# The first batch's selective scans in wide units of 1024 columns, their three elementwise steps all on VectorE

## The chip, the cores and the metric

One core of a Trainium2 chip runs the whole kernel in one launch. The metric is the device time of that launch in microseconds (us). The engines are TensorE (PE, matmul), VectorE (DVE), ScalarE (ACT), GpSimd (POOL) and SyncE (SP, which here only issues DMAs). Each engine takes its instructions in the order in which they were written for it, and they wait for one another by semaphores.

## The reference

The input is `x` (4 batches of 512 tokens, 256 wide) and a context (4 x 1601 x 256). One decoder layer is computed: a Mamba block, a cross-attention of 16 heads in which the context and the latents are keys and values, and a mixture of experts; after each a residual sum and a layernorm. The part that matters here is the Mamba scan:

```python
xs = silu(conv(xs) + conv_b);  dt = softplus(dt @ W_dt.T + b_dt)
dA  = exp(dt[..., None] * A)                      # 512 channels x 16 states x 512 tokens
dBx = dt[..., None] * Bm[:, :, None, :] * xs[..., None]
h_t = dA_t * h_(t-1) + dBx_t                      # recurrence over the 512 tokens
y_t = sum over the 16 states of h_t * C_t;   y = (y + xs * D) * silu(z) @ W_out.T
```

The attention needs `layer_norm(context) @ Wkv` and `layer_norm(x after Mamba) @ Wq`, in a precision near fp32: every weight is split into a high part and the rest (`raw - high`), and a product is the sum of three.

## The kernel before, in words

Three blocks follow each other: `mamba` (projections, convolution, dt; it leaves dt, dt*x, B, C and the gate in DRAM), `attention` and `experts`. The scans aren't done in `mamba`: each batch's scans run inside `attention`. Those of the next three batches run beside the attention of the batch before, on POOL and DVE, and nothing of them changes here. Those of the first batch (called batch 0 here) have no attention to run beside, and fill the opening of the `attention` block, from the first loads to the first scores. This opening is what the change touches.

A unit of a scan is one state n (of NS = 16) and one tile c of 128 channels (of CT = 4): 128 partitions x 512 tokens, so NU = 64 units a batch. A unit takes: `decays` on ACT (L833: exp of dt times a scale per partition), `times_b` on POOL (L731: dt*x times the row B_n), `scan` on DVE (L942: the recurrence, then from L953 the product with the row C_n, in place, unless `on_pool(u)`; for u = 24, 26, ... that product is `times_c` on POOL, L741), and `sum_state` on PE (L1208: one fp32 matmul with the identity, which adds the unit to the sum of its channel tile in PSUM). Rings of buffers: FR = 3 for decays and dbx each, FS = 4 for the states. The scan of unit u waits for the sum of unit u - FS. The rows B_n and C_n are one tile `bc` of 2 buffers, broadcast from DRAM by SP (`load_bc`).

The order of all that is one list written out by `first()` (L370), which every engine walks, each making its own part of an item: D (decays, times_b), H (scan), C (times_c, the sum), and between them the preparation of the context, in equal steps: S (row statistics, DVE), A (their sums, DVE, and a power on POOL), N (normalise two row tiles, DVE), T (turn them, PE, and high part, ACT), U (low part, DVE), W (split one weight, `split` at L761: both halves on POOL; 12 of them), then V and K (products of the context, PE, evicted by DVE, for K by ACT and DVE). There are 57 such items, the last nine V0 to V5 and K0 to K2. In the split, the first write of every third weight waits until SP has stored the tile of the split weights before it in DRAM (`w_stored`).

After the list's scans: `gate_first` (DVE, L958, it waits for the last sums and for the gate's DMA), the output projection, layernorms, Q and the remaining K, the first row maxima, and from there the attention of all heads.

Of the kernel before, what the change touches and what calls it, by code (L numbers as in the profile page):

```python
# [22 lines left out]
P = 128  # L23
# [9 lines left out]
KEPT = {}  # L33
# [268 lines left out]
FR = 3  # L302
FS = 4
# [4 lines left out]
NU = CT * NS  # L308
# [61 lines left out]
def first():  # L370


    early = [("S", 0, t) for t in range(CTX_T)] + [("A", 0, i) for i in range(2)]
    early += [("W", 0, i) for i in range(3 * NG)]
    n_ctx = CTX_T // 2 + 1
    for i in range(n_ctx + 1):
        early += ([("N", 0, i)] if i < n_ctx else []) + ([("T", 0, i - 1)] if i > 0 else [])
        early += [("U", 0, i - 2)] if i > 1 else []
    early += [("U", 0, n_ctx - 1)]
    early += [("V", 0, i) for i in range(V_EARLY)] + [("K", 0, i) for i in range(3)]  # L380

    splits, others = [x for x in early if x[0] == "W"], [x for x in early if x[0] in "SANTU"]
    head = []
    for i, x in enumerate(others):
        head += [x] + (splits[i // 2:i // 2 + 1] if i % 2 == 1 else [])
    head += splits[len(others) // 2:]
    early = head + [x for x in early if x[0] in "VK"]
    made, done = [], 0
    for u in range(NU + 3):
        for kind, later in (("H", 1), ("D", 0), ("C", 2)):  # L390
            if 0 <= u - later < NU:
                made.append((kind, 0, u - later))
        while done < len(early) and done * (NU - 4) < (u + 1) * len(early):
# [21 lines left out]
def attention(nc, ctx_rows, g1, b1, g2, b2, wq, wkv, wo, x1):  # L415
    w_dram = nc.dram_tensor("a_w_split", (NG, P, 6 * KD * GW), F32, kind="Internal").ap()

    with ExitStack() as ctx:
# [39 lines left out]
        decay_first, dbx_first, state_first = parts(early, 0, FR), parts(early, FR, FR), parts(early, 2 * FR, FS)  # L458
        w_out_first = early[:, (2 * FR + FS) * S:(2 * FR + FS + 2) * S].rearrange("p (c d) -> p c d", d=DM)
# [53 lines left out]
        seen_pool = sem("a_seen_pool")  # L513
        seen_dve = sem("a_seen_dve")
# [31 lines left out]
        def unit(b, u):  # L546
            return b * NU + u
# [4 lines left out]
        def on_pool(u):  # L552

            return u >= 24 and u % 2 == 0

        def by_pool(u):
            return sum(on_pool(i) for i in range(u + 1))

        def ring_of(b):
            return FR if b == 0 else 2  # L560

        def dtu_of(b, c, i):
            if c < 2:
                return dtu[:, c, i]
            return p[:, 2 * (c - 2) + i] if b == 0 else dtu_two[:, 2 * (c - 2) + i]

        def inputs(b, u):
            i = u % ring_of(b)
            return (decay_first[:, i], dbx_first[:, i]) if b == 0 else (decay[:, i], dbx[:, i])

        def state_of(b, u):
            return state_first[:, u % FS] if b == 0 else state[:, u % 2]

        def wait_inputs_free(engine, b, u):
            r = ring_of(b)
            if u >= r:
                engine.wait_ge(scanned, unit(b, u) - r + 1)
            elif b > 0:
                engine.wait_ge(turned_low, b * len(PREP))

        def wait_multiplied(engine, b, u):
            if b > 0:
                engine.wait_ge(seen_ready, late(b, u) + 1)
            else:
                if by_pool(u):
                    engine.wait_ge(seen_pool, by_pool(u))
                engine.wait_ge(seen_dve, u + 1 - by_pool(u))

        @block.sync
        def _(sp):  # L590
# [17 lines left out]

            def load_bc(b, n):
                i = b * NS + n  # L610
                if n >= 2:
                    wait_multiplied(sp, b, CT * (n - 1) - 1)
                elif b > 0:
                    sp.wait_ge(gated, b * CT)
                sp.dma_start(bc[:, i % 2].rearrange("p i s -> p (i s)"),
                             KEPT["bc"][BATCHES[b], n].partition_broadcast(P)).then_inc(bc_loaded[i % 2], 16)

            def load_gate(b):
                wait_multiplied(sp, b, NU - 1)
                sp.dma_start(gate.rearrange("p c s -> p (c s)"), KEPT["z"][BATCHES[b]]).then_inc(gate_loaded, 16)  # L620
                if b > 0:
                    sp.wait_ge(scanned, unit(b, NU))
                sp.dma_start(w_out_first if b == 0 else w_out,
                             KEPT["w_out_t"].rearrange("(c p) d -> p c d", p=P)).then_inc(w_out_loaded, 16)
# [23 lines left out]
            load_bc(0, 0)  # L648
            load_batch(0)
            load_rows(0)  # L650
            load_bc(0, 1)
# [4 lines left out]
            for what in BEFORE:  # L656
                if what[0] == "W" and what[2] >= 1 and what[2] + 1 < 3 * NG:
                    load_raw(what[2] + 1)
                elif what[0] == "W" and what[2] == 3 * NG - 1:
                    sp.wait_ge(raw_split, 3 * NG)  # L660
                    sp.dma_start(w_dram[0], wt[:].rearrange("p i k n -> p (i k n)").bitcast(F32)).then_inc(w_stored, 16)
                elif what[0] == "C" and what[2] % CT == CT - 1 and what[2] // CT + 2 < NS:
                    load_bc(0, what[2] // CT + 2)
# [46 lines left out]
        def _(pool):  # L710
# [20 lines left out]
            def times_b(b, u):  # L731
                n, c = divmod(u, CT)
                i = b * NS + n
# [5 lines left out]
                nc.gpsimd.tensor_tensor(inputs(b, u)[1], dtu_of(b, c, 1), bc[:, i % 2, 0], ALU.mult).then_inc(dbx_ready, 1)  # L739

            def times_c(b, u):  # L741
                n, c = divmod(u, CT)
                i = b * NS + n
                if b == 0:
                    if on_pool(u):
                        pool.wait_ge(scanned, u + 1)
                        nc.gpsimd.tensor_tensor(state_of(b, u), state_of(b, u), bc[:, i % 2, 1], ALU.mult).then_inc(seen_pool, 1)
                    return
# [23 lines left out]
            for what in BEFORE:  # L772
                if what[0] == "D":
                    times_b(*what[1:])
                elif what[0] == "C":
                    times_c(*what[1:])
                elif what[0] == "W":
                    split(what[2])
                elif what in POW:
                    make_rstd(what)  # L780
# [12 lines left out]
        def _(act):  # L793
# [39 lines left out]
            def decays(b, u):  # L833
                n, c = divmod(u, CT)
                wait_inputs_free(act, b, u)
                if u == 0:
                    act.wait_ge(dtu_loaded, 32 * (b + 1))
                nc.scalar.activation(inputs(b, u)[0], dtu_of(b, c, 0), ACT.Exp,
                                     scale=a_neg[:, c, n:n + 1]).then_inc(decay_ready, 1)

# [4 lines left out]
            def make(what):  # L845
# [6 lines left out]
                elif what[0] == "D":  # L852
                    decays(*what[1:])
# [30 lines left out]
        def _(dve):  # L884
            dve.wait_ge(a_set, 1)
            nc.vector.tensor_scalar(a_neg[:], a_neg[:], -1.0, None, ALU.mult).then_inc(a_set, 1)
            dve.wait_ge(consts_set, 1)
            nc.vector.memset(wo_sb[DH:DH + 1], 0.0)
# [53 lines left out]
            def scan(b, u):  # L942
                n, c = divmod(u, CT)
                i = b * NS + n
                dve.wait_ge(decay_ready, unit(b, u) + 1)
                dve.wait_ge(dbx_ready, unit(b, u) + 1)
                if b == 0 and u >= FS:
                    dve.wait_ge(summed, u - FS + 1)
                elif b > 0 and u >= 2:
                    dve.wait_ge(y_added, late(b, u) - 1)  # L950
                dA, dB = inputs(b, u)
                nc.vector.tensor_tensor_scan(state_of(b, u), dA, dB, 0.0, ALU.mult, ALU.add).then_inc(scanned, 1)  # L952
                if b == 0 and not on_pool(u):  # L953
                    dve.wait_ge(bc_loaded[i % 2], 16 * (i // 2 + 1))
                    dve.wait_ge(scanned, u + 1)
                    nc.vector.tensor_tensor(state_of(b, u), state_of(b, u), bc[:, i % 2, 1], ALU.mult).then_inc(seen_dve, 1)

            def gate_first():  # L958
                dve.wait_ge(y_loaded, 16)
                dve.wait_ge(gate_loaded, 16)  # L960
                for c in range(CT):
                    dve.wait_ge(summed, NU - CT + c + 1)
# [90 lines left out]
            def make(what):  # L1053
# [15 lines left out]
                elif kind == "H":  # L1069
                    scan(*what[1:])  # L1070
# [28 lines left out]
        def _(pe):  # L1099
# [108 lines left out]
            def sum_state(u):  # L1208
                wait_multiplied(pe, 0, u)
                n, c = divmod(u, CT)  # L1210
                nc.tensor.matmul(sums(c), ident[:], state_first[:, u % FS], start=(n == 0), stop=(n == NS - 1)).then_inc(summed, 1)

# [817 lines left out]
```

## Time and profile before

| | |
|---|---|
| median of 3 runs | 3302.6 us (3299.16 to 3303.39) |
| profiled execution, its own time | 3303.27 us |
| its span | 3301.5 us |
| busy over the span | PE 91%, DVE 62%, ACT 41%, POOL 33% |
| mean granted TensorE clock | 0.943 |

The span is the time from the first to the last instruction; the own time of the execution is 1.8 us more. Busy shares are means over stages with different limits: PE is nearly full from the first scores on, but not in the opening, which lies between about 199.8 us (first product of the scans) and 435 us (last product with C).

### The profile page before, as it was taken

To read this page: it belongs to the slowest core of one execution; us is meant where nothing else is said; L and a number is where in the kernel's file an instruction comes from. 1 tells how busy PE (TensorE), PEld (TensorE's weight loads), DVE (VectorE), ACT (ScalarE), POOL (GpSimd) and SP (SyncE) were. 2 spreads that over 40 slices of the span, in tenths; PEclk is the share of its full clock that TensorE was granted. 3 is DMA by queue.
4 is the path that set the end of the run, shared out by engine and by line. 5 is a ranking of instruction groups with operands and counts; after the bars stand their busy time and mean duration, and the time that the engine had idled before them with its cause. 6 is when DMAs were issued, how large, how long until landed. Compare 5 with 4: busy or idle time off the path is not lost. (4 is left out here: it accounts for less than half of the span.)

```text
span 3301.5 us, 33908 instructions
## 1 busy us (share of the span) xinstructions
PE 3000.6 (91%) x11590; PEld 1862.5 (56%) x11590; DVE 2040.4 (62%) x3415; ACT 1346.4 (41%) x2307; POOL 1084.0 (33%) x824
## 2 busy tenths in 40 slices
PE   6624659999999999999999999999999999899997
PEld 2201326656566665656565665666566665576666
DVE  4668867776756777775677777565555545352225
ACT  4521215454535445453645445344434344321121
POOL 0047726676500466660036666200000000102213
PEclk8856769999999999999999999999999999799998
DMA  2342122121212212121122112110101100321112
GB/s 100 122 157 89 57 88 77 33 61 33 61 34 58 80 37 68 33 61 41 36 71 68 54 34 62 53 36 14 36 14 43 36 18 16 129 81 48 52 41 69
DMA packets 73182, 189.83 MB, mean 57 GB/s; under 512 B 8388, under 2 KB 42312, under 8 KB 64440
## 3 DMA queue, kind: packets, MB, share of 16 engines
q1 hardware_dynamic: 69176, 178.37, 17.8%
q0 software_dynamic: 3408, 9.31, 1.0%
q8 instruction: 95, 1.56, 0.2%
q14 instruction: 71, 0.58, 0.1%
q10 hardware_dynamic: 432, 0.01, 0.0%
HBM read 120.39 MB, written 32.64 MB: 46 GB/s over the span
## 5 line engine op out<-in xcount | busy, mean ns | idle before, releaser
L1253 PE MATMUL a_o<-a_p,a_vals 128*65 128x512 f32 (+1 forms) x2176 | 1113.5, 593 | 0.0
L860 ACT ACTIVATE a_p<-a_st 128x512 f32<-128x512 f32 (+1 forms) x1088 | 649.2, 597 | 1127.1 <-PE a_st L1241 1119.0
L1018 DVE TENSOR_REDUCE a_maxes<-a_mx 128x1 f32<-128x512 f32 x1024 | 683.0, 686 | 219.6 <-PE a_mx L1171 213.1
L1241 PE MATMUL a_st<-a_q,a_kone 65*128 65x512 f32 (+1 forms) x1088 | 430.6, 396 | 0.0
L750 POOL TENSOR_TENSOR a_shared<-a_shared,a_bc 128x512 f32<-128x512 f32 x192 | 252.6, 1316 | 383.5 <-DVE a_shared L952 383.5
L1253 PEld LDWEIGHTS a_o<-a_p,a_vals 128*65 128x65 f32 (+1 forms) x2176 | 284.3, 137 | 103.4 <-issue 1.8
L1240 PE MATMUL a_st<-a_q,a_keven 128*128 128x512 f32 (+1 forms) x544 | 326.0, 599 | 0.7 <-issue 0.7
L1240 PE MATMUL a_st<-a_q,a_kodd 128*128 128x512 f32 (+1 forms) x544 | 314.7, 578 | 0.0
L729 POOL TENSOR_TENSOR a_erstd<-a_emv,a_half 128x4 f32<-128x4 f32 x8 | 8.1, 1014 | 916.1 <-DVE a_emv L1044 916.1
L1171 PE MATMUL a_mx<-a_kodd,a_q 128*128 128x512 f32 x512 | 298.3, 599 | 7.3 <-DVE a_maxes L1018 6.2
L952 DVE TENSOR_TENSOR_SCAN a_shared<-a_shared 128x512 f32<-128x512 f32 x192 | 287.7, 1500 | 13.1 <-POOL a_shared L739 12.0
L1171 PE MATMUL a_mx<-a_keven,a_q 128*128 128x512 f32 x512 | 277.0, 588 | 12.9 <-DVE a_maxes L1018 10.2
L1241 PEld LDWEIGHTS a_st<-a_q,a_kone 65*128 65x128 f32 (+1 forms) x1088 | 202.1, 186 | 152.8 <-issue 128.7
L754 POOL TENSOR_TENSOR a_y<-a_y,a_shared 128x512 f32<-128x512 f32 x192 | 255.6, 1331 | 15.3
L1124 PE MATMUL a_ring<-a_kvh,a_wt 128*128 128x512 f32 (+1 forms) x768 | 229.7, 381 | 5.1 <-DVE a_kvl L984 2.9
L1011 DVE COPY a_vals<-a_ring 128x512 f32<-128x512 f32 (+2 forms) x160 | 97.3, 608 | 186.4 <-PE a_ring L1124 184.3
L739 POOL TENSOR_TENSOR a_shared<-a_dtu,a_bc 128x512 f32<-128x512 f32 x96 | 146.6, 1528 | 169.2 <-DMA a_bc<-m_kept_bc 169.2
L1171 PEld LDWEIGHTS a_mx<-a_keven,a_q 128*128 128x128 f32 x512 | 97.9, 191 | 162.9 <-DVE a_maxes L1018 64.6
L1124 PE MATMUL a_ring<-a_wt,a_kvh 128*128 128x256 f32 (+1 forms) x1088 | 177.6, 286 | 0.0
L1240 PEld LDWEIGHTS a_st<-a_q,a_keven 128*128 128x128 f32 (+1 forms) x544 | 101.4, 186 | 132.5 <-issue 94.2
L1660 DVE TENSOR_TENSOR e_gate<-e_silu,e_h 128x512 f32<-128x512 f32 x71 | 48.7, 687 | 199.1 <-ACT e_silu L1522 180.0
L1124 PEld LDWEIGHTS a_ring<-a_wt,a_kvh 128*128 128x128 f32 (+1 forms) x1088 | 160.1, 189 | 18.4 <-issue 3.8
(243 smaller groups left out, 4539.7 us busy)
## 6 DMA issues: line engine op xcount, KB each, us to landing
a_bc<-m_kept_bc SPq DMA_DIRECT2D x64, 512.0 KB, 3.7
a_wt<-a_w_split SPq DMA_DIRECT2D x15, 1536.0 KB, 9.8
a_kone<-a_keven SPq DMA_DIRECT2D x32, 528.5 KB, 4.5
a_kone<-a_kodd SPq DMA_DIRECT2D x32, 528.5 KB, 4.2
e_wall<-in_w_t_dram SPq DMA_DIRECT2D x27, 512.0 KB, 5.5
a_shared<-in_ctx_dram SPq DMA_DIRECT2D x4, 1536.0 KB
a_w_split<-a_wt SPq DMA_DIRECT2D x4, 1536.0 KB, 8.5
e_y_dram<-e_y_row SPq DMA_DIRECT2D x39, 128.0 KB, 1.7
```

Source lines behind the costliest of these rows:

```text
L739: nc.gpsimd.tensor_tensor(inputs(b, u)[1], dtu_of(b, c, 1), bc[:, i % 2, 0], ALU.mult).then_inc(dbx_ready, 1)
L750: nc.gpsimd.tensor_tensor(state[:, u % 2], state[:, u % 2], bc[:, i % 2, 1], ALU.mult).then_inc(seen_ready, 1)
L754: nc.gpsimd.tensor_tensor(y[:, c], y[:, c], state[:, u % 2], ALU.add).then_inc(y_added, 1)
L860: nc.scalar.activation(p[0:r, s % 4], st[0:r, s % 2], ACT.Exp, scale=SCALE).then_inc(exp_done, 1)
L952: nc.vector.tensor_tensor_scan(state_of(b, u), dA, dB, 0.0, ALU.mult, ALU.add).then_inc(scanned, 1)
L1011: o = nc.vector.tensor_copy(vals[0:r, t * HG:(t + w) * HG, 0:DH], made)
L1018: nc.vector.reduce_max(maxes[:, c, t:t + 1], mx[:, i % 2], AX_X).then_inc(mx_max, 1)
L1124: mm = nc.tensor.matmul(out, x(k), y(k), start=(j == 0), stop=(j == len(terms) - 1))
L1171: mm = nc.tensor.matmul(mx[:, i % 2], qd[of(g)][:, t * P:(t + 1) * P], kk[:, c * 512:(c + 1) * 512], start=True, stop=True)
L1240: nc.tensor.matmul(st[0:r, s % 2], keys_of(g)[:, kt * P:kt * P + r], qd[of(g)], start=True, stop=False)
L1241: nc.tensor.matmul(st[0:r, s % 2], k_one[g % 2][0:DH + 1, kt * P:kt * P + r], qm[of(g)][0:DH + 1, :], start=False, stop=True).then_inc(st_ ...
L1253: nc.tensor.matmul(ps_o[0:DH + 1, g % 2], vals[0:r, kt * HG + j, :], p[0:r, s % 4], start=(kt == 0), stop=(kt == KT - 1)).then_inc(pv_done, 1)
```

## The change

The 64 units become NW = 32 wide units of CW = 2 channel tiles each: one state, 1024 columns, scanned as one (the decay of the first token of each half is a constant zero, so that the second half starts from zero). Both products are on DVE: that with B writes straight into the state's buffer, and the scan works there in place. The rings are FR = 2 wide decays, FS = 3 wide states and FB = 3 rows of B and C. The split's high half goes to ACT, POOL keeps the low half. On PE a wide unit has two matmuls and one semaphore step. The list has D, H, C and the same 57 items in the same order, spread over 32 rounds.

```diff
-FR = 3
-FS = 4
+NU = CT * NS
+CW = 2
+NW = NU // CW
+FR = 2
+FS = 3
+FB = 3
...
-    for u in range(NU + 3):
-        for kind, later in (("H", 1), ("D", 0), ("C", 2)):
-            if 0 <= u - later < NU:
-                made.append((kind, 0, u - later))
-        while done < len(early) and done * (NU - 4) < (u + 1) * len(early):
+    for w in range(-1, NW + 1):
+        made += [("D", 0, w + 1)] if w + 1 < NW else []
+        made += [("H", 0, w)] + ([("C", 0, w - 1)] if w > 0 else [])
+        while done < len(early) and done * (NW - 2) < (w + 2) * len(early):
...
+            def load_bc_first(n):
+                if n >= FB:
+                    sp.wait_ge(seen_first, CW * (n - FB + 1))
...
             def split(i):
                 which = i % 3
-                if which == 0 and i > 0:
-                    pool.wait_ge(w_stored, 16 * (i // 3))
-                pool.wait_ge(raw_loaded[i % 2], 16 * (i // 2 + 1))
+                pool.wait_ge(raw_high, i + 1)
                 raw = o_sb[:, i % 2].rearrange("p (k n) -> p k n", n=GW)
-                nc.gpsimd.tensor_copy(wt[:, 2 * which], raw).then_inc(raw_high, 1)
-                pool.wait_ge(raw_high, i + 1)
...
+            def decays_first(w):
+                n, k = divmod(w, CW)
+                if w >= FR:
+                    act.wait_ge(scanned, w - FR + 1)
...
+                for i in range(CW):
+                    c = k * CW + i
+                    e = nc.scalar.activation(decay_first[:, w % FR, i, 1:S], dtu_first(k, 0)[:, i, 1:S], ACT.Exp,
+                                             scale=a_neg[:, c, n:n + 1])
+                e.then_inc(decay_ready, 1)
+
+            def split_high(i):
+                which = i % 3
+                if which == 0 and i > 0:
+                    act.wait_ge(w_stored, 16 * (i // 3))
+                act.wait_ge(raw_loaded[i % 2], 16 * (i // 2 + 1))
+                nc.scalar.activation(wt[:, 2 * which], o_sb[:, i % 2].rearrange("p (k n) -> p k n", n=GW),
+                                     ACT.Copy).then_inc(raw_high, 1)
...
+            def scan_first(w):
+
+                if w + 1 < NW:
+                    n, k = divmod(w + 1, CW)
+                    if w == -1:
+                        dve.wait_ge(dtu_loaded, 32)
+                    if k == 0:
+                        dve.wait_ge(bc_first[n % FB], 16 * (n // FB + 1))
+                    if w + 1 >= FS:
+                        dve.wait_ge(summed, w + 1 - FS + 1)
+                    nc.vector.tensor_tensor(state_first[:, (w + 1) % FS], dtu_first(k, 1),
+                                            rows_first(n)[:, 0:1].to_broadcast([P, CW, S]), ALU.mult).then_inc(dbx_first, 1)
+                if 0 <= w < NW:
+                    dve.wait_ge(decay_ready, w + 1)
+                    dve.wait_ge(dbx_first, w + 1)
+                    h = state_first[:, w % FS].rearrange("p c s -> p (c s)")
+                    nc.vector.tensor_tensor_scan(h, decay_first[:, w % FR].rearrange("p c s -> p (c s)"), h, 0.0, ALU.mult,
+                                                 ALU.add).then_inc(scanned, 1)
+                if w >= 1:
+                    dve.wait_ge(scanned, w)
+                    h = state_first[:, (w - 1) % FS]
+                    nc.vector.tensor_tensor(h, h, rows_first((w - 1) // CW)[:, 1:2].to_broadcast([P, CW, S]),
+                                            ALU.mult).then_inc(seen_first, 1)
...
+            def sum_state(w):
+                wait_multiplied(pe, 0, w)
+                n, k = divmod(w, CW)
+                for i in range(CW):
+                    mm = nc.tensor.matmul(sums(k * CW + i), ident[:], state_first[:, w % FS, i], start=(n == 0), stop=(n == NS - 1))
+                mm.then_inc(summed, 1)
```

## Rows read from the trace of the kernel before

**Rows 1.** The page's busy times over the whole span.
```profile
PE 3000.6 (91%) x11590; PEld 1862.5 (56%) x11590; DVE 2040.4 (62%) x3415; ACT 1346.4 (41%) x2307; POOL 1084.0 (33%) x824
```

**Rows 2.** Windows view (PE, PEld, DVE, ACT, POOL busy, PE clock, DMA): the scans, then early attention.
```profile
204.00:435.00 231.00, 125.89 (x241) 48.40 (x242) 200.84 (x167) 56.22 (x88) 166.87 (x106) 0.65 0.23 74
...
520.00:540.00 20.00, 20.00 (x74) 11.95 (x73) 12.56 (x15) 14.35 (x25) 17.04 (x12) 1.00 0.07 27
```

**Rows 3.** Groups by line and shape, 195 to 440 us (busy, mean ns, idle before, releasers).
```profile
L952 DVE TENSOR_TENSOR_SCAN a_early<-a_early 128x512 f32<-128x512 f32 x64 | 109.7, 1724 | 18.8 <-POOL a_early L739 8.7 <-issue 6.9 <-ACT a_early L838 2.9
L956 DVE TENSOR_TENSOR a_early<-a_early,a_bc 128x512 f32<-128x512 f32 x44 | 58.3, 1326 | 4.6
L1211 PE MATMUL a_st<-a_early,a_ident 128*128 128x512 f32 x64 | 55.3, 970 | 89.3 <-DVE a_early L956 66.0 <-POOL a_early L747 23.1
```

**Rows 4.** Timeline, first units (start us, us, engine, line).
```profile
203.89 0.43 DVE L905 BATCH_NORM_STATS2 a_stats<-a_shared 128x6 f32<-128x256 f32 x1 [10.90 <-DMA a_shared<-in_ctx_dram]
204.23 1.21 DVE L952 TENSOR_TENSOR_SCAN a_early<-a_early 128x512 f32<-128x512 f32 x1
...
205.54 0.69 DVE L956 TENSOR_TENSOR a_early<-a_early,a_bc 128x512 f32<-128x512 f32 x1
...
206.38 4.24 PE L1211 MATMUL a_st<-a_early,a_ident 128*128 128x512 f32 x4 [43.31 <-DVE a_early L956]
```

**Rows 5.** Timeline near 251 us: DVE while POOL is busy.
```profile
251.18 2.28 DVE L952 TENSOR_TENSOR_SCAN a_early<-a_early 128x512 f32<-128x512 f32 x1
...
252.34 3.85 POOL L739 TENSOR_TENSOR a_early<-a_dtu,a_bc 128x512 f32<-128x512 f32 x2
...
253.57 1.50 DVE L956 TENSOR_TENSOR a_early<-a_early,a_bc 128x512 f32<-128x512 f32 x1
```

**Rows 6.** One line, L236: an fp32 product of 2048 columns (min/median/max ns).
```profile
L236 DVE TENSOR_TENSOR m_dt<-m_w,m_relu x4: 2291/2291/2293, 55.8 to 175.0; 128x2048 f32<-128x2048 f32 x4
```

**Rows 7.** Timeline of PE: two units' sums back to back (x4), idle before them.
```profile
305.77 3.78 PE L1211 MATMUL a_o<-a_early,a_ident 128*128 128x512 f32 x4 [4.11 <-POOL a_early L747]
...
312.18 1.98 PE L1211 MATMUL a_st<-a_early,a_ident 128*128 128x512 f32 x4 [1.77 <-POOL a_early L747]
322.14 3.78 PE L1211 MATMUL a_o<-a_early,a_ident 128*128 128x512 f32 x4 [7.98 <-POOL a_early L747]
...
351.09 3.03 PE L1211 MATMUL a_o<-a_early,a_ident 128*128 128x512 f32 x4 [2.45 <-POOL a_early L747]
...
423.66 3.62 PE L1211 MATMUL a_o<-a_early,a_ident 128*128 128x512 f32 x4 [3.66 <-POOL a_early L747]
```

**Rows 8.** Timeline, a V item: its product on PE, its copy on DVE.
```profile
396.41 1.04 PE L1124 MATMUL a_ring<-a_wt,a_kvh 128*128 128x256 f32 x4
...
398.00 0.40 PE L1124 MATMUL a_ring<-a_wt,a_kvl 128*128 128x256 f32 x2
...
398.43 0.69 DVE L1011 COPY a_vals<-a_ring 128x512 f32<-128x512 f32 x1 [0.98 <-PE a_ring L1124]
```

**Rows 9.** Timeline, a K item on PE, ACT and DVE.
```profile
406.73 1.03 PE L1124 MATMUL a_ring<-a_kvh,a_wt 128*128 128x512 f32 x2
...
408.73 0.59 ACT L829 ACTIVATE a_keven<-a_ring 64x512 fp32r<-64x512 f32 x1 [6.84 <-PE a_ring L1124]
...
410.33 0.69 DVE L1000 TENSOR_TENSOR a_keven<-a_ring,a_keven 64x512 fp32r<-64x512 f32 x1
```

**Rows 10.** Timeline, a store of split weights and the split behind it; an exponent.
```profile
271.58 0.32 SPq L615 DMA_DIRECT2D a_bc<-m_kept_bc  x1
...
272.42 0.47 SPq L646 DMA_DIRECT2D a_w_split<-a_wt  x1
...
281.07 0.61 POOL L767 CAST a_wt<-a_osb 128x512 fp32r<-128x512 f32 x1 [12.00 <-DMA a_w_split<-a_wt]
281.76 1.26 POOL L769 TENSOR_TENSOR a_wt<-a_osb,a_wt 128x512 fp32r<-128x512 f32 x1
...
285.59 0.72 ACT L838 ACTIVATE a_early<-a_dtu,a_aneg 128x512 f32<-128x512 f32 x1 [9.83 <-DVE a_early L952]
```

**Rows 11.** Timeline, the end of the scans.
```profile
433.52 1.50 DVE L956 TENSOR_TENSOR a_early<-a_early,a_bc 128x512 f32<-128x512 f32 x1
...
435.10 0.32 SPq L620 DMA_DIRECT2D a_bc<-m_kept_z  x1
...
439.97 1.29 DVE L963 TENSOR_TENSOR a_y<-a_st,a_y 128x512 f32<-128x512 f32 x2 [4.95 <-DMA a_bc<-m_kept_z]
```

More of the change, by code:

```diff
@@ L301 @@
 LAG = 3
-FR = 3
-FS = 4
+NU = CT * NS
[4 more added lines that the diff above has]
+FB = 3
 V_EARLY = 6
 NX = TT * (len(KC) - 1) + 1
-NU = CT * NS
 U_STEP = 2.85
@@ L457, in attention @@
         w_out = shared[:, 8 * S:10 * S].rearrange("p (c d) -> p c d", d=DM)
-        decay_first, dbx_first, state_first = parts(early, 0, FR), parts(early, FR, FR), parts(early, 2 * FR, FS)
-        w_out_first = early[:, (2 * FR + FS) * S:(2 * FR + FS + 2) * S].rearrange("p (c d) -> p c d", d=DM)
+        wide = lambda t, at, n: t[:, at * CW * S:(at + n) * CW * S].rearrange("p (i c s) -> p i c s", c=CW, s=S)
+        decay_first, state_first = wide(early, 0, FR), wide(early, FR, FS)
+        bc_third = early[:, (FR + FS) * CW * S:(FR + FS) * CW * S + 2 * S].rearrange("p (j s) -> p j s", s=S)
+        w_out_first = early[:, (FR + FS) * CW * S + 2 * S:(FR + FS) * CW * S + 4 * S].rearrange("p (c d) -> p c d", d=DM)
         a_neg = sb("a_aneg", [P, CT, NS])
@@ L512, in attention @@
         gate_loaded = sem("a_gate_loaded")
-        seen_pool = sem("a_seen_pool")
-        seen_dve = sem("a_seen_dve")
+        bc_first = [sem(f"a_bc_first{i}") for i in range(FB)]
+        dbx_first = sem("a_dbx_first")
+        seen_first = sem("a_seen_first")
+        zeroed = sem("a_zeroed")
         summed = sem("a_summed")
@@ L546, in unit, with dtu_first, rows_first @@
         def unit(b, u):
-            return b * NU + u
+            return u if b == 0 else NW + (b - 1) * NU + u
         def late(b, u):
             return (b - 1) * NU + u
[L552 to L560, printed above, removed]
-        def dtu_of(b, c, i):
[L563 to L572, printed above, removed]
+        def dtu_of(b, c, i):
+            return dtu[:, c, i] if c < 2 else dtu_two[:, 2 * (c - 2) + i]
+        def dtu_first(k, i):
+            return dtu[:, :, i] if k == 0 else p[:].rearrange("p (c i) s -> p c i s", i=2)[:, :, i]
+        def rows_first(n):
+            return bc[:, n % FB] if n % FB < 2 else bc_third
         def wait_inputs_free(engine, b, u):
[L575 to L578, printed above, removed]
+            if u >= 2:
+                engine.wait_ge(scanned, unit(b, u) - 1)
+            else:
                 engine.wait_ge(turned_low, b * len(PREP))
@@ L584, in wait_multiplied @@
             else:
-                if by_pool(u):
-                    engine.wait_ge(seen_pool, by_pool(u))
-                engine.wait_ge(seen_dve, u + 1 - by_pool(u))
+                engine.wait_ge(seen_first, u + 1)
         @block.sync
@@ L607, in load_wo @@
                 sp.dma_start(wo_sb[0:DH, n % 2, :, 0:DM], wo_src[:, n % NG * HG:(n % NG + 1) * HG]).then_inc(wo_loaded, 16)
+            def load_bc_first(n):
+                if n >= FB:
+                    sp.wait_ge(seen_first, CW * (n - FB + 1))
+                sp.dma_start(rows_first(n).rearrange("p j s -> p (j s)"),
+                             KEPT["bc"][BATCHES[0], n].partition_broadcast(P)).then_inc(bc_first[n % FB], 16)
             def load_bc(b, n):
-                i = b * NS + n
+                i = (b - 1) * NS + n
                 if n >= 2:
                     wait_multiplied(sp, b, CT * (n - 1) - 1)
-                elif b > 0:
+                else:
                     sp.wait_ge(gated, b * CT)
@@ L618, in load_gate @@
             def load_gate(b):
-                wait_multiplied(sp, b, NU - 1)
+                wait_multiplied(sp, b, (NU if b > 0 else NW) - 1)
                 sp.dma_start(gate.rearrange("p c s -> p (c s)"), KEPT["z"][BATCHES[b]]).then_inc(gate_loaded, 16)
                 if b > 0:
-                    sp.wait_ge(scanned, unit(b, NU))
+                    sp.wait_ge(scanned, unit(b, NU - 1) + 1)
                 sp.dma_start(w_out_first if b == 0 else w_out,
@@ L646, in load_raw @@
                     sp.dma_start(w_dram[n + 1], wt[:].rearrange("p i k n -> p (i k n)").bitcast(F32)).then_inc(w_stored, 16)
-            load_bc(0, 0)
+            load_bc_first(0)
             load_batch(0)
             load_rows(0)
-            load_bc(0, 1)
+            load_bc_first(1)
+            load_bc_first(2)
             sp.wait_ge(ones_set, 1)
@@ L661, in _ @@
                     sp.dma_start(w_dram[0], wt[:].rearrange("p i k n -> p (i k n)").bitcast(F32)).then_inc(w_stored, 16)
-                elif what[0] == "C" and what[2] % CT == CT - 1 and what[2] // CT + 2 < NS:
-                    load_bc(0, what[2] // CT + 2)
+                elif what[0] == "C" and what[2] % CW == CW - 1 and what[2] // CW + FB < NS:
+                    load_bc_first(what[2] // CW + FB)
             load_gate(0)
@@ L732, in times_b @@
                 n, c = divmod(u, CT)
-                i = b * NS + n
+                i = (b - 1) * NS + n
                 wait_inputs_free(pool, b, u)
@@ L738, in times_b @@
                     pool.wait_ge(bc_loaded[i % 2], 16 * (i // 2 + 1))
-                nc.gpsimd.tensor_tensor(inputs(b, u)[1], dtu_of(b, c, 1), bc[:, i % 2, 0], ALU.mult).then_inc(dbx_ready, 1)
+                nc.gpsimd.tensor_tensor(dbx[:, u % 2], dtu_of(b, c, 1), bc[:, i % 2, 0], ALU.mult).then_inc(dbx_ready, 1)
             def times_c(b, u):
                 n, c = divmod(u, CT)
[L743 to L748, printed above, removed]
+                i = (b - 1) * NS + n
                 pool.wait_ge(scanned, unit(b, u) + 1)
@@ L772, in _ @@
             for what in BEFORE:
[L773 to L777, printed above, removed]
+                if what[0] == "W":
                     split(what[2])
@@ L837, in decays @@
                     act.wait_ge(dtu_loaded, 32 * (b + 1))
-                nc.scalar.activation(inputs(b, u)[0], dtu_of(b, c, 0), ACT.Exp,
+                nc.scalar.activation(decay[:, u % 2], dtu_of(b, c, 0), ACT.Exp,
                                      scale=a_neg[:, c, n:n + 1]).then_inc(decay_ready, 1)
+            def decays_first(w):
+                n, k = divmod(w, CW)
+                if w >= FR:
+                    act.wait_ge(scanned, w - FR + 1)
+                elif w == 0:
+                    act.wait_ge(dtu_loaded, 32)
+                    act.wait_ge(zeroed, 1)
+                for i in range(CW):
[10 more added lines that the diff above has]
+                                     ACT.Copy).then_inc(raw_high, 1)
             def turn_row(g):
@@ L852, in make @@
                 elif what[0] == "D":
-                    decays(*what[1:])
+                    if what[1] == 0:
+                        decays_first(what[2])
+                    else:
+                        decays(*what[1:])
+                elif what[0] == "W":
+                    split_high(what[2])
             def exp(s):
@@ L887, in _ @@
             dve.wait_ge(consts_set, 1)
+            nc.vector.memset(decay_first[:, :, :, 0:1], 0.0).then_inc(zeroed, 1)
             nc.vector.memset(wo_sb[DH:DH + 1], 0.0)
@@ L942, in scan @@
             def scan(b, u):
-                n, c = divmod(u, CT)
-                i = b * NS + n
                 dve.wait_ge(decay_ready, unit(b, u) + 1)
[L946 to L949, printed above, removed]
+                dve.wait_ge(dbx_ready, late(b, u) + 1)
+                if u >= 2:
                     dve.wait_ge(y_added, late(b, u) - 1)
-                dA, dB = inputs(b, u)
@@ L952, in scan @@
[L952 to L956, printed above, removed]
+                nc.vector.tensor_tensor_scan(state[:, u % 2], decay[:, u % 2], dbx[:, u % 2], 0.0, ALU.mult,
+                                             ALU.add).then_inc(scanned, 1)
@@ new lines, in scan_first @@
+            def scan_first(w):
[14 more added lines that the diff above has]
+                    nc.vector.tensor_tensor_scan(h, decay_first[:, w % FR].rearrange("p c s -> p (c s)"), h, 0.0, ALU.mult,
+                                                 ALU.add).then_inc(scanned, 1)
+                if w >= 1:
[3 more added lines that the diff above has]
+                                            ALU.mult).then_inc(seen_first, 1)
@@ L961, in gate_first @@
                 for c in range(CT):
-                    dve.wait_ge(summed, NU - CT + c + 1)
+                    dve.wait_ge(summed, NW - CT // CW + c // CW + 1)
                     s = nc.vector.tensor_tensor(y[:, c], sums(c), y[:, c], ALU.add)
@@ L1069, in make @@
                 elif kind == "H":
-                    scan(*what[1:])
+                    if what[1] == 0:
+                        scan_first(what[2])
+                    else:
+                        scan(*what[1:])
                 elif kind == "P":
@@ L1206, in project_out @@
                                  wo_sb[0:DH + 1, g // HG % 2, g % HG], start=True, stop=True).then_inc(ring_full, 1)
[L1208 to L1211, printed above, removed]
+            def sum_state(w):
[4 more added lines that the diff above has]
+                mm.then_inc(summed, 1)
             def make(what):
```

## The prediction

> **What bounds the kernel now.** I read the page's busy times first [rows 1]: PE is busy 91% of the span, so work on other engines costs time only where PE is not the limit. The windows view then says where that is [rows 2]: from 204 to 435 us PE is busy 125.9 of 231 us, while at 520 us it is busy all of 20. So a microsecond gained or lost before the first scores moves all that follows by a microsecond. The change touches nothing behind them, and I carry the shift of the opening to the end unchanged.
>
> In the opening DVE is the busiest, 200.8 of 231 us [rows 2]. The groups by line show the kind of bound [rows 3]: the 64 scans had only 18.8 us of idle before them, 8.7 of it for POOL's product, and none for PE: nobody waits for the sums. But a scan's mean is 1.72 us, and one with POOL at rest took 1.21 [rows 4]; beside POOL it took 2.28, and the product 1.50 instead of 0.69 [rows 4, 5]. So DVE's time is partly contention with POOL. The stretch of scans ends at 433.52 + 1.50 = 435.0 us, and the gate's DMA goes out right behind it, at 435.10 [rows 11].
>
> **Part 1, the work on DVE.** A product of 2048 columns takes 2.29 us [rows 6], one of 512 takes 0.69 [rows 4]: (2.29 - 0.69)/1536 = 1.04 ns a column and 0.16 us fixed, so 1024 columns take 1.22 us. No other length of a scan is in the trace. Bounds: 1.21 + 512 columns at the product's rate = 1.74 us, and 2 x 1.21 = 2.42 us. With the product's fixed 0.16 us a scan has 2.05 ns a column, and 1024 take 2.26 us, which I take. A round on DVE is product with B, scan, product with C: 1.22 + 2.26 + 1.22 = 4.70 us, 32 of them 150 us. Alone, that beats today: 64 scans and 44 products are busy 109.7 + 58.3 = 168.0 us [rows 3], and the POOL products that slowed them go.
>
> The Trainium skill (SBUF — State Buffer, "Who interferes with whom") says that a DVE operation with two SBUF inputs and a GpSimd one that reads SBUF exclude each other for the whole instruction. The rows at 251 us agree: 2.28 against 1.21. By that rule alone the change is a gain; it is the third case below.
>
> **Part 2, the new wait.** This is the step that decides. In round w DVE makes the product with B of unit w+1, then the scan of w, then the product with C of w-1. The first writes the buffer of the state ring of three in which unit w-2 lay, so it waits for the sum of w-2 (`summed` >= w-1). But the product with C of w-2 was DVE's last instruction of the round before. So in each round DVE stands still while PE adds up a whole wide unit. Before, a scan waited for the sum of four units back, which cost nothing. What is queued behind the waiting product: all of DVE, thus ACT's next exponent and PE's next sum.
>
> The price of one such gap: from the end of the product to PE's start 0.15 us (205.54 + 0.69 to 206.38 [rows 4]), then two fp32 matmuls, which are x4 in the records, and the way back, for which I take 0.05 us. Four in a row took 4.24 us from a cold start [rows 4] and 3.78, 3.78 and 3.62 us after idle of 4.11, 7.98 and 3.66 us; 3.03 after 2.45 us; and 1.98 at the full clock [rows 7]. So the bounds are 1.98 and 4.24 us. In the new rhythm PE is idle for DVE's 4.70 us between two sums, or about 3.6 where it turns a context tile; after idle of 3.66 us and more it began at the lower clock (1.2 GHz) each time. I take 3.80, and a gap of 4.00 us.
>
> DVE's small items of a round (S, N, U, at most two) come behind the product with C and before the waiting product: one such statistic is 0.43 us [rows 4], two low parts about 1.4, so they lie inside the gap and cost nothing. If the gap shrank to 2.2 us they still would.
>
> The gaps: units 3 to 31 wait, rounds 2 to 30, so 29 x (4.70 + 4.00) = 252.3 us.
>
> **Part 3, V and K behind the gap.** At the end of the list a round has two V items: on PE they come behind the sum, and DVE must copy them before its next product. A V product takes 396.41 to 398.40 = 1.99 us, its copy 0.69 [rows 8]. So a gap with two is 0.15 + 3.80 + 1.99 + 1.99 + 0.69 + 0.05 = 8.7, 4.7 more than 4.0; three such rounds, 14.0 us. A K product takes about 1.96 us, then two ACT evictions of 0.59 and two DVE ones of 0.69 [rows 9], with their steps 1.2 and 1.4. The round with two K's: 3.95 + 2 x 1.96 + 1.2 + 1.4 = 10.5, 6.5 more; that with one: 8.5, 4.5 more. Together 25.0 us. Before, such waits lay in part beside PE's other work; here DVE has nothing of its own left to do.
>
> **Part 4, what moves to ACT and POOL.** ACT takes 12 high halves (the cast was 0.61 on POOL [rows 10]; as much on ACT, below 1.3 us each). ACT's exponents for unit w+1 start when the scan of w-1 ends and take 2 x 0.72 [rows 10]; the high half and POOL's low half of 1.26 us then end about 3.5 us after that scan, so inside the gap, and POOL's low half meets no DVE product. Cost 0; if it did meet one, 12 x 1.1 = 13 us, the difference in [rows 4, 5]. The wait for a store of split weights moves to ACT, ahead of exponents. SP sends the store behind a load of B and C that waits for a product with C; from that load to the split behind the store were 281.07 - 271.58 = 9.5 us [rows 10]. With 0.3 before, the high half and the exponents the next decay is ready 12 us after that product; its scan is due after gap, round, gap and product, 4.0 + 4.7 + 4.0 + 1.2 = 13.9 us. Hidden, with 1.9 us to spare. The third buffer of rows gives SP's loads of B and C about three rounds' lead. PE's and ACT's own work stays below the rounds.
>
> **The sum.** The context rows land at 203.89 as before, and DVE has the first product made by then; two statistics end at 204.7. Round 0 has 1.22 + 2.26 + 0.42 = 3.9: 208.6. Round 1, no wait: 213.3. Rounds 2 to 30: 465.6. V and K: 490.6. Rounds 31 and 32, scan and two products: 495.3. Today 435.0. The shift is +60.3 us; behind it everything repeats, the gate's DMA (4.95 us of idle) ahead of the last sums too [rows 11]. On the profiled execution's own time 3303.3 + 60.3 = 3363.6; the median of the runs is 0.7 below that execution, so 3363.
>
> **The rivals.**
>
> Second case, the sums run at the full clock. Busy in one stretch of 3.8 us a round, PE might hold it over the idle; the sum at 312 us took 1.98 after 1.77 us of idle. Then a gap is 2.2 us: 29 x 1.8 = 52 less, a shift of +8, 3311 us. Against it: every row with more than 3.6 us of idle. The Trainium skill (TensorE: Matmul & The Clock Gate, the table of Part 1) gives 1.2 GHz as the state after idling; taken strictly for each whole sum that is 4.24 us, 29 x 0.44 = 13 us more than my sum, 3376.
>
> Third case, on the other side: the wait on the sums isn't felt, and DVE is bound by its own work, free of POOL. That needs PE to be done before DVE asks; it decides from the point where a sum is shorter than DVE's small items of a round, below about 1 us. Then 204.7 + 3.9 + 31 x 4.70 = 354.3, some 23 us of small items and copies without contention and 8 for V and K: 385, a shift of -50, 3253 us. Against it stand the wait as written and the shortest sum in the trace, 1.98.
>
> Fourth, ACT is late: stores take longer than 9.5 us and hold the exponents, as POOL's copy was held 12.0 us [rows 10]. Three stores with up to 7 us each, about 20 on top: 3383.
>
> **The numbers.** A difference of 0.2% (6.6 us) is what a measurement tells from none. Chances: 0.70 for my sum, with its own range of 3340 to 3378 (a sum of a unit between 3.03 and 4.24 us); 0.10 for the second; 0.07 for the third; 0.13 for the fourth or for POOL's contention. The range 3322 to 3390 leaves out the second's core and the third. Slower: 0.90. Same: 0.03, the low edge of the second. Faster: 0.07.
>
> **What would show it.** The profile after should have DVE products with B of 1.22 us preceded by about 4 us of idle released by PE's sum, nearly 30 times (100 us and more); scans of about 2.26 us; sums of a wide unit at 3.6 to 4.2 us; PE idle of 4.7 between them; the last product with C at about 495 us; the same chain behind. I am wrong if DVE's idle before that product is small, if a wide scan costs far from 2.26 us, or if the idle in front of DVE is for ACT's exponents.

## The result and the profile after

The changed kernel takes 3356.6 us (median of 4 runs, 3355.0 to 3359.4), against 3303.0 us in the same session: a ratio of 1.0163 (95% interval 1.015 to 1.0176), 54 us slower. The forecast was 3363 with a range of 3322 to 3390. The profiled execution took 3359.4 us; its page, to be held against [rows 1]:

```profile
span 3357.7 us, 33686 instructions
...
PE 3008.1 (90%) x11590; PEld 1871.9 (56%) x11590; DVE 2013.6 (60%) x3404; ACT 1351.6 (40%) x2319; POOL 936.0 (28%) x728
```

DVE and POOL work less than before, PE and ACT 7.6 and 5.2 us more, and the span is 56.2 us longer. So it isn't work that was added; something stands still. Windows view of both, 204 to 350 us (PE, PEld, DVE, ACT, POOL busy), the kernel before:

```profile
204.00:350.00 146.00, 72.91 (x92) 21.54 (x92) 123.68 (x110) 33.45 (x51) 110.31 (x71) 0.60 0.30 99
```

and the changed one:

```profile
204.00:350.00 146.00, 61.69 (x76) 21.16 (x76) 92.55 (x87) 31.64 (x53) 20.67 (x12) 0.59 0.28 86
```

DVE fell from 123.7 to 92.6 of 146 us, in the stretch where it was the busiest engine. The waits view of the changed kernel, 195 to 495 us (who waited for whom: total, times, longest), names what it waits for:

```profile
DVE a_early L971 <- PE a_st L1242: 41.9, 13, 3.9
ACT a_wt L843 <- DMA a_w_split<-a_wt: 37.3, 3, 17.6
DVE a_early L971 <- PE a_o L1242: 34.9, 10, 3.9
...
DVE a_vals L1038 <- PE a_ring L1154: 19.0, 6, 6.2
DVE a_keven L1027 <- ACT a_kodd L814: 14.0, 2, 7.2
```

L971 is the product with B, L1242 the sum on PE. Before, nobody waited for a sum; now DVE does 23 times, 76.8 us in all, and stands still for 33 us more where V and K come behind it. One round in the timeline shows it whole (start us, us, engine, line, idle before and its releaser):

```profile
242.01 1.23 DVE L971 TENSOR_TENSOR a_early<-a_dtu,a_bc 128x1024 f32<-128x1024 f32 x1 [3.55 <-PE a_o L1242]
243.16 2.28 DVE L977 TENSOR_TENSOR_SCAN a_early<-a_early 128x1024 f32<-128x1024 f32 x1
245.36 1.20 DVE L982 TENSOR_TENSOR a_early<-a_early 128x1024 f32<-128x1024 f32 x1
...
246.61 3.78 PE L1242 MATMUL a_st<-a_early,a_ident 128*128 128x512 f32 x4 [4.71 <-DVE a_early L982]
...
250.43 1.23 DVE L971 TENSOR_TENSOR a_early<-a_p,a_bc 128x1024 f32<-128x1024 f32 x1 [3.21 <-PE a_st L1242]
```

DVE and PE take turns: DVE's three steps to 246.56, PE's sum from 246.61 to 250.39, DVE again at 250.43. The round is 8.42 us. The last products with C (x2) and the gate's load, the rows that answer to [rows 11]:

```profile
485.94 2.33 DVE L982 TENSOR_TENSOR a_early<-a_early,a_bc 128x1024 f32<-128x1024 f32 x2
...
488.30 0.32 SPq L616 DMA_DIRECT2D a_bc<-m_kept_z  x1
```

The scans end at 488.3 instead of 435.0 us, 53.3 later. The first scores' matmul started at 499.6 before and starts at 553.0 now, 53.4 later. The other 3 us of the span come and go behind it; the medians differ by 53.6.

### The profile page after: what moved, and what is told of

The parts are those of the page before. It is cut to its first block and busy times, and to the rows that moved or that the text cites. A ratio compares the mean times of both kernels' runs of the same rounds, so it can differ in the third digit from the quotient of the medians.

```text
span 3357.7 us, 33686 instructions
## 1 busy us (share of the span) xinstructions
PE 3008.1 (90%) x11590; PEld 1871.9 (56%) x11590; DVE 2013.6 (60%) x3404; ACT 1351.6 (40%) x2319; POOL 936.0 (28%) x728
## 5 line engine op out<-in xcount | busy, mean ns | idle before, releaser
L1201 PE MATMUL a_mx<-a_keven,a_q 128*128 128x512 f32 x512 | 276.9, 588 | 12.7 <-DVE a_maxes L1045 10.2
```

The costliest lines, as they stand in the source:

```text
L1201: mm = nc.tensor.matmul(mx[:, i % 2], qd[of(g)][:, t * P:(t + 1) * P], kk[:, c * 512:(c + 1) * 512], start=True, stop=True)
```

## The experiments

Each ratio is that of a kernel's runs to those of the kernel before in the same session; differences between kernels of two sessions are those of their ratios, times 3303 us.

**e1, the product with B last.** The same three steps of DVE, in another order.

```diff
 def scan_first(w):
-    if w + 1 < NW: (product with B of w + 1)
     if 0 <= w < NW: (scan of w)
     if w >= 1: (product with C of w - 1)
+    if w + 1 < NW: (product with B of w + 1)
```

> The changed kernel with one edit: in each round DVE makes the product with B of unit w+1 last, behind the scan of w and the product with C of w-1, instead of first. The ring of three states and all waits stay. Theory (DVE stands still for PE's sum of the unit whose buffer it writes): the sum of w-2 then has DVE's 4.5 us of scan and products to run beside, a plain round falls from about 8.5 us to 4.5 and its small items (0.8), some 24 rounds save 3.2 us, the five rounds with V and K about 1.1 each: the last product with C at about 405 us instead of 488, time about 3273 us. Rival (the wait only hides the next limit: ACT's exponents behind the stores of split weights, SP's loads of rows): the idle moves to the scan, waiting for ACT, and the time stays above 3340 us.

Measured: 3287.6 us, ratio 0.9954 (0.9937 to 0.997): 69 us less than the changed kernel, by one of the three steps moved. DVE's waits for L1242 are gone from the view. The last scan starts at 411.3 us. It missed the forecast by 15 us, and the waits view (195 to 495 us) says by what for most of it, in its second line:

```profile
DVE a_vals L1038 <- PE a_ring L1154: 20.7, 9, 5.7
DVE a_early L967 <- ACT a_early L834: 12.7, 6, 4.8
DVE a_keven L1027 <- ACT a_kodd L814: 11.0, 2, 5.7
```

So the rival was right in a small part: the wait for the sums had covered 12.7 us of waits for ACT's exponents. The waits behind V and K (20.7 and 11.0 us) are no new ones: the changed kernel has them with 19.0 and 14.0.

**e5, four state buffers,** order as in the changed kernel.

```diff
-FS = 3
+FS = 4
-w_out_first = early[:, (FR + FS) * CW * S + 2 * S:(FR + FS) * CW * S + 4 * S]
+w_out_first = early[:, 0:2 * S]
```

> The changed kernel, order of DVE's three steps unchanged, with a state ring of four buffers instead of three (the output weights are loaded over the decays, which are dead by then, so that the fourth fits). Theory: the wait on the sums goes by depth as it went by order; the product with B shows no idle for PE. The rounds with V and K keep their length (they wait for PE with nothing else to do), about 8 us more in all than with B last: about 3295 us. Rival (the gain of the reordered kernel came from DVE's order itself and not from the ring): near 3357 us.

Measured: 3290.5 us, 0.9972 (0.9962 to 0.9981), 63 us less than the changed kernel. In its waits view no product waits for a sum; DVE's scans wait 14.3 us for ACT, much as in e1. (A form with the fourth buffer in one of the keys' buffers, e2, gave no time.) Two different edits, depth and order, remove the same wait and give nearly the same time. It was the distance in the ring, not a side effect of either edit.

**e3, half a sum.** From the third unit on the second channel tile of each wide unit is left out of the sum.

```diff
-for i in range(CW):
+for i in range(CW if n == 0 else 1):
     mm = nc.tensor.matmul(sums(k * CW + i), ident[:], state_first[:, w % FS, i], ...)
```

> The changed kernel, but from the third unit on the sum on PE has one matmul instead of two: the second channel tile of each wide unit is left out of the sum. Theory: the gap in front of the product with B is PE's sum, so it falls from 3.78 to 2.08 us; 27 gaps and the V and K rounds with them, 31 x 1.7: 53 us less, about 3304 us. If the gap were latency of semaphores or a DVE effect: under 10 us less, above 3345.

Measured: 3321.7 us, 1.0058 (1.0041 to 1.0075), 35 us less. The plain rounds fell from 8.42 to 6.71 us, by 1.71, as one matmul of two would. Timeline, the sum of a round and the product that waits for it:

```profile
242.31 2.07 PE L1242 MATMUL a_st<-a_early,a_ident 128*128 128x512 f32 x2 [4.70 <-DVE a_early L982]
244.42 1.23 DVE L971 TENSOR_TENSOR a_early<-a_p,a_bc 128x1024 f32<-128x1024 f32 x1 [1.50 <-PE a_st L1242]
244.69 0.63 ACT L843 ACTIVATE a_wt<-a_osb 128x512 fp32r<-128x512 f32 x1 [15.66 <-DMA a_w_split<-a_wt]
...
246.57 2.35 DVE L977 TENSOR_TENSOR_SCAN a_early<-a_early 128x1024 f32<-128x1024 f32 x1 [0.93 <-ACT a_early L834]
```

The forecast was 53 us less. Of the missing 18, 7 are a wrong count in the expectation: the sums of units 0 and 1 are still whole, so 27 gaps shrink and not 31. Some 5 lie in the rounds before V and K, around the three stores above all (8.9, 10.5 and 9.5 us, where 9.6, 9.4 and 9.4 had been): with a shorter gap the store's wait on ACT shows, here 0.93 us, and POOL's splits and its power, held up together, meet DVE's operations or keep it waiting. The five rounds with V and K fell by 5.4 us in all and not by 8.5, which is 3 more. The rest I did not trace.

**e4, a warm PE.** PE makes 66 matmuls more.

```diff
     mm.then_inc(summed, 1)
+    if w < 22:       # w = 0 waits for y's load first
+        for i in range(3):
+            nc.tensor.matmul(mx[:, 0], ident[:], y[:, 0], start=True, stop=True)
```

> The changed kernel, and behind each of the first 22 sums PE makes three more fp32 matmuls of 512 columns into an unused PSUM bank (their result isn't read), so that it idles about 1.3 us instead of 4.6 between sums. Theory (a sum costs 3.78 us since PE begins it at the lower clock after idling): once the clock is up a sum takes 1.98 us, 22 rounds x 1.8 = up to 40 us less, 3318 us, while PE does 66 matmuls more. Rival (the sum's time is not the clock's, or PE's extra work delays the next sum): no gain, or up to 22 x 1.5 = 33 us more.

Measured: 3327.7 us, 1.008 (1.0062 to 1.0098), 27 us less with more work. Timeline of its PE:

```profile
265.29 1.98 PE L1244 MATMUL a_o<-a_early,a_ident 128*128 128x512 f32 x4 [2.06 <-DVE a_early L982]
...
272.00 1.98 PE L1244 MATMUL a_st<-a_early,a_ident 128*128 128x512 f32 x4 [2.16 <-DVE a_early L982]
```

The same sum takes 1.98 instead of 3.78 us, and a plain round 6.65. The granted clock was 1.00 during the first of these sums (265.29 to 267.27 us, windows view) and 0.50 during that of the round shown above (246.60 to 250.40). So of the gap of 3.9 us, 1.8 are the lower clock at which PE starts after the 4.6 us that it waits for DVE. The kernel pays for its own idleness.

Up to 40 us had been forecast. The 22 rounds from 216.33 us on take 161.8 us, where they took 190.1: 28 less. Six of the 22 sums still took 2.43 to 3.78 us, and the rounds at the three stores stayed long (10.1, 10.4 and 8.9 us).

**e10, the whole split back on POOL,** in the changed kernel.

```diff
 def split(i):
+    (wait for w_stored and raw_loaded, as before)
+    nc.gpsimd.tensor_copy(wt[:, 2 * which], raw).then_inc(raw_high, 1)
```

> The changed kernel with one part undone: the high halves of the 12 splits are back on POOL, the wait for the store with them, so that no exponent stands behind it. Theory: in the changed kernel ACT's waits are hidden by the gaps for PE's sum, so this part is worth nothing either way; POOL's cast ends before DVE's next product or takes a port from it as the low half did in five rounds: 3357 us, within 6. Rival (ACT's standing still of 37 us at the stores is felt): 10 us or more less.

Measured: 3357.8 us, 1.0173 (1.0156 to 1.019). No clear difference, where the two intervals leave room for a few us: ACT's 37 us behind stores cost the changed kernel nothing that the runs can tell.

**e6, e1 with three decays.**

```diff
-FR = 2
+FR = 3
```

> The kernel with B last, and three decay buffers instead of two. There the scan waited 12.7 us for ACT's exponents, in rounds of 10 to 11 us at the three stores of split weights. Theory: that is ACT held by the store's wait ahead of the exponents; one more decay in store covers about one more round (4.7 us) at each: 8 to 12 us less, about 3277 us. Rival (the scan waits for ACT's own work or the DMA of rows): no change, 3288 us.

Measured: 3282.6 us, 0.995 (0.9931 to 0.997), no clear difference to e1. The theory fell: the scan still waited 12.4 us for ACT. Timeline:

```profile
236.77 0.63 ACT L843 ACTIVATE a_wt<-a_osb 128x512 fp32r<-128x512 f32 x1 [20.19 <-DMA a_w_split<-a_wt]
237.31 1.32 ACT L834 ACTIVATE a_early<-a_dtu,a_aneg 128x511 f32<-128x511 f32 x2
...
238.66 2.29 DVE L967 TENSOR_TENSOR_SCAN a_early<-a_early 128x1024 f32<-128x1024 f32 x1 [4.84 <-ACT a_early L834]
```

ACT did wait for the store, but the exponents that a third buffer could have held stood behind that wait in the list. A buffer doesn't help an engine that takes its work in order and isn't asked for it earlier.

**e7, e6 with V and K evicted a round later by DVE.** 

```diff
-for what in BEFORE:
+for what in order:      # BEFORE, with V0-V5 and K0-K2 held back until the next H is made
     if what == ("P", 0, 0):
         gate_first()
```

> The kernel with B last and three decays, and in it DVE evicts the nine items V0 to V5 and K0 to K2 one round later than PE makes them (only DVE's order changes). Theory: the five rounds of 10.5 to 12.7 us with V and K are DVE waiting behind PE's sum and products; with the product and scan of the next round to do meanwhile they take about 6.5: some 24 us less than the kernel before it, about 3253 us. Rival (PE's own work bounds these rounds): under 8 us less.

Measured: 3257.5 us, 0.9869 (0.9849 to 0.9888), 25 us below e6. The rounds of 10.5 to 12.4 us became 5.6 to 7.4, and of e6's 21.2 us of waits behind V these are left:

```profile
DVE a_vals L1039 <- PE a_ring L1166: 7.4, 4, 5.7
```

**e9, e7 with the exponents two rounds ahead.**

```diff
+    made.append(("D", 0, 0))
     for w in range(-1, NW + 1):
-        made += [("D", 0, w + 1)] if w + 1 < NW else []
+        made += [("D", 0, w + 2)] if w + 2 < NW else []
```

> The kernel with B last, three decays and V and K a round later, and in the list ACT's exponents two rounds ahead of the scan instead of one. The third buffer alone did not take the 12 us for which scans wait for ACT: the list keeps the exponents of two units on behind the split that waits for its store. Theory: with those exponents written ahead of it, the wait for ACT falls from 12 us to under 4: some 9 us less, about 3248 us. Rival (the store's landing bounds DVE in another way, through PE's V items or the rows' loads): no change.

Measured: 3246.9 us, 0.984 (0.9824 to 0.9857), 10 us below e7; this is what the third buffer was for. It beats both kernels: 53 us less than the one before with the same work as the changed one. Its windows row, 204 to 350 us:

```profile
204.00:350.00 146.00, 86.53 (x177) 35.14 (x178) 142.82 (x128) 51.55 (x87) 29.51 (x13) 0.73 0.33 109
```

and its last products with C:

```profile
376.79 2.33 DVE L974 TENSOR_TENSOR a_early<-a_early,a_bc 128x1024 f32<-128x1024 f32 x2
```

DVE is busy 142.8 of 146 us, and the scans end at 379.1. This is the third case of the prediction, for which I had worked out 385 us and 3253.

**e8 and e11, narrow units, both products on DVE.** The kernel before, with its 64 units, but POOL makes no product for the first batch. In e8 the product with C is made a unit later, in e11 at once.

```diff
 def scan(b, u):
+    if b == 0: (product with B of u + 1; of 0 and 1 at u = 0)
     (scan of u)
+    e8:  product with C of u - 1
+    e11: product with C of u
```

> The kernel before (64 units of 512 columns, rings of 3 and 4, splits on POOL) with one part of the change: both products of the first batch's scans on DVE, that with B a unit ahead, that with C a unit behind. Theory: contention with POOL was DVE's loss; a narrow unit takes 0.61 + 1.13 + 0.61 = 2.35 us, 64 of them 150 us, small items 23, waits for V, K and stores some 30: scans end near 407 us instead of 435, about 3275 us. Rival (taking 20 + 64 products onto DVE costs more than the contention did): above 3303 us.

> The kernel with narrow units and both products on DVE, but the product with C of a unit right behind its scan, as in the kernel before, instead of a unit later. There the splits, rows and turns were done 16 us earlier than in the kernel before, but each of the nine V and K items then held DVE for 7 us. Theory: that was PE's sum, which came a unit's product later and stood ahead of the V product; with it made at once the V and K items wait some 2 us less each, and the scans end about 20 us earlier: near 3297 us. Rival (the nine items wait because DVE has less work to do beside them, whatever the order): within 6 us of 3320.

Measured: e8 3319.9 us, 1.0057 (1.0038 to 1.0076); e11 3270.5 us, 0.9909 (0.9892 to 0.9925). My theory for e8 missed by 45 us. Its first V copy was at 372.5 us where the kernel before had it at 388.3, so taking the products from POOL had gained 16 us by then. But from then on each V item came 6.8 to 7.7 us after the one before. Timeline of e8:

```profile
382.66 2.08 PE L1221 MATMUL a_o<-a_early,a_ident 128*128 128x512 f32 x2 [3.10 <-DVE a_early L966]
383.74 1.84 PE L1134 MATMUL a_ring<-a_wt,a_kvh 128*128 128x256 f32 x4
...
387.33 0.69 DVE L1021 COPY a_vals<-a_ring 128x512 f32<-128x512 f32 x1 [4.73 <-PE a_ring L1134]
```

With C at once, the same stretch in e11:

```profile
372.21 1.13 PE L1221 MATMUL a_st<-a_early,a_ident 128*128 128x512 f32 x2 [0.51 <-DVE a_early L966]
...
372.77 1.04 PE L1134 MATMUL a_ring<-a_wt,a_kvh 128*128 128x256 f32 x4
...
375.13 0.68 DVE L1021 COPY a_vals<-a_ring 128x512 f32<-128x512 f32 x1
```

The sum starts a scan earlier, PE idles 0.51 us before it and not 3.10, the sum takes 1.13 us and not 2.08, and the copy waits for nothing. Windows view (the granted clock stands behind POOL's busy time) from the first V copy to the last K operation, e8:

```profile
372.50:437.00 64.50, 33.69 (x94) 22.39 (x94) 26.29 (x35) 8.55 (x14) 0.00 (x0) 0.65 0.05 16
```

and e11:

```profile
359.80:387.70 27.90, 20.94 (x96) 13.91 (x96) 26.71 (x36) 8.81 (x15) 0.00 (x0) 1.00 0.11 38
```

The whole was worth 49 us, where I expected 23: 36.6 of them here, 12.7 by the first V copy. I had counted the order and not the clock that comes with it; which part each of the two has, no run separates. e11 also shows that the part "both products on DVE" alone is a gain of 30 us on the kernel before.

## Why the prediction was right

**The new wait** is the mechanism, as forecast: the product with B stood still for the sum of unit w-2, whose product with C ended the round before. e1 and e5 remove it in two ways for 69 and 63 us, e3 and e4 scale it by PE's time alone.

**Its price** was nearly right: a gap of 4.00 us was forecast and measures 250.43 - 246.56 = 3.87; the sum itself 3.80 against 3.78. The rows of sums after long idle [rows 7] carried this term, and e4 confirms that they show the clock. One of the bounds was misread: the 4.24 us "from a cold start" [rows 4] are two units' sums, and the second waited for its product with C, which ended at 207.80 + 0.69 = 208.49 us. In sums that ran at the lower clock throughout, two fp32 matmuls took 3.75 or 3.78 us, so that was already the top, and the case of 3376 us, priced with 4.24, had nothing under it. The term itself doesn't rest on that row. The second case, a clock that holds over the idle, did not occur by itself; e4 had to force it.

**A round of DVE** was 0.15 us too long: 4.70 against 242.01 to 246.56 = 4.55. The scan of 1024 columns takes 2.28 us (2.26 forecast) and the products 1.23 and 1.20 (1.22 twice), but each starts 0.08 us before the recorded end of the one before it. I had added durations where starts should be subtracted.

**POOL's contention** was put at 0 and costs about 5 us: in round 1 and in four later ones (9.33 to 9.55 us instead of 8.42) one operation of DVE takes some 1.05 us longer. A fifth long round (9.39) waits for POOL's power. The high half on ACT doesn't always end early enough for POOL's low half to fit the gap. That these two errors nearly cancel is luck: the 22 rounds from 216.96 to 407.02 us are 8.64 each, forecast 8.70.

**V and K** were forecast as 5 x 8.70 + 25.0 = 68.5 us for their five rounds; from the product with B at 407.02 to that at 470.86 they took 63.8. Of the difference 1.4 is the shorter round, five times; 1.7 is the second V of a pair, whose copy comes 1.42 us after the first where I had taken 1.99; and PE starts these products up to 1 us before the recorded end of the sum (450.93 against 451.92). These 4.7 us are most of the 7 by which the end of the scans (488.3 against 495.3) was missed.

**The stores on ACT** were forecast as hidden with 1.9 us to spare. e10 finds no cost of them, and e1 and e3, which shorten a round, show that the room was small.

**The marker that was wrong in form:** "nearly 30 times" 4 us of idle before the product with B. There were 23, of 3.3 us on average, because the small items of a round and the V and K copies take their place in the gap, and the wait is then booked on them.

**The third case** was the only one with a faster kernel, and the end of its scans was priced well (e9: 379 us for 385), but it needed more than the wait's removal: e1 alone left 44 us of other waits, 32 for V and K, which the changed kernel had too, and 12.7 for ACT, which the gaps had covered.

## What to carry to other kernels

Count a ring's distance in the consumer's steps, not in buffers: where the last step of a round releases the buffer that the first step of the next round fills, the whole latency of the engine in between is paid in every round, and moving one step to the end can be worth as much as one more buffer. PE, when it is made to wait in each round, may also start at its lower clock, and so lengthen the wait of the others. When a stall goes, look in the same trace for the waits that it covered, and add depth only together with an order that asks for the work earlier.

## What I had not expected of the hardware

Two fp32 matmuls of 512 columns (x4 in the records) took 3.78 us in most of the rounds after 4.6 us of idle and 1.98 after 2.06 or 2.16 us of it with PE busy before (e4): the same two levels as in [rows 7], now repeated at will. The 66 matmuls more made the whole kernel 27 us faster. The Trainium skill (TensorE: Matmul & The Clock Gate, the table of Part 1) has 1.2 GHz as the state after idling and 2.4 GHz as the busy one, and these rows agree: the granted clock was 0.50 in the sums of 3.78 us and 1.00 in those of 1.98.

3.78 is a little under twice 1.98: by these two, 0.18 us of either doesn't scale with the clock (an estimate). Where the clock rose within a sum, it took less than 3.78, as the 3.62 and 3.03 us of [rows 7], at a mean of 0.54 and 0.63. The higher level was granted in the changed kernel too, but in part while PE stood idle. Windows view from one sum to the end of the next (238.18, the sum before the round shown above):

```profile
238.18:241.70 3.52, 3.52 (x4) 1.17 (x4) 0.28 (x1) 0.00 (x0) 0.00 (x0) 0.50 0.75 170
241.72:245.12 3.40, 0.18 (x1) 0.00 (x0) 3.11 (x2) 0.00 (x0) 0.00 (x0) 1.00 1.00 409
245.15:246.60 1.45, 0.00 (x0) 0.00 (x0) 1.45 (x3) 0.00 (x0) 0.00 (x0) 0.50 0.54 229
246.60:250.40 3.80, 3.78 (x4) 1.18 (x4) 0.62 (x2) 2.82 (x5) 1.27 (x1) 0.50 0.01 3
```

The clock rose as PE's sum ended and had fallen again before the next began.
